# A four-layer graph network on one core: the SBUF start of the adjacency matrices and of the attention matrix is shifted by 64 bytes against the other matmul operands

## The chip, the cores and the metric

The program runs on one core of a Trainium2 chip. Its time is the device time of one execution in microseconds (us); before the change the median of three runs is 2620.7 us (2620.21 to 2622.87). A lower number is better.

## The reference

The input is 64 graphs of 256 nodes with 512 features, and for each graph a 256x256 matrix `adj`. Four layers follow one another, each with a layer norm, a clip at zero and a residual addition:

```
h = relu(layernorm(x))
L0:  Wh = h W;  e = leaky_relu(Wh a1 + (Wh a2)^T);  p = softmax(where(adj > 0.5, e, -9e15), axis=1)
     x = x + elu(p Wh)
L1:  Ah = adj + I;  d = rsqrt(rowsum(Ah));  x = x + relu((d Ah d) h K1 + bias)
L2:  x = x + relu((adj h) K2) * (h has a non-zero in the row)
L3:  x = x + relu(h Wa^T + (adj h / max(rowsum(adj), 1e-6)) Wb^T)
```

Everything is float32 (W, K1, K2, Wa and Wb are 512x512).

## The kernel before

**Split operands.** Every matmul operand is held twice, as a high part (a cast to fp32r) and a low part (what the cast lost). One product is three matmuls: high by high, high stationary by low moving, low stationary by high moving (`product`, lines 273 to 279, all recorded as L277). The first operand of each pair is the stationary one (128 columns, loaded by LDWEIGHTS), the second is the moving one. In the profile's names the moving operand stands first: `O<-w_hi,t_lo` is a matmul that writes O, with w_hi moving and t_lo stationary.

**Matmuls of a layer.** Layers 0 to 2 first gather, then project. `gather` (line 313 on) makes T = (h^T)(adjacency) with a piece of `h_hi`/`h_lo` stationary and 256 columns of `a_hi`/`a_lo` moving (in layer 0 of `p_hi`/`p_lo`, the attention matrix): 4 feature blocks x 2 node blocks x 3 = 24 matmuls 256 wide. `project` (line 347 on) makes O with `t_hi`/`t_lo` stationary and the 512 columns of a weight moving: 24 matmuls 512 wide. Layer 3 turns this round. `transpose_h` transposes h with 8 matmuls (L310, `ident` moving, h stationary); `project_first` multiplies by a weight (T from w and ht, 24 matmuls 512 wide); `gather_last` makes the own term (X from w and ht, 24 of 512), then the gather with `a_hi`/`a_lo` stationary and `t_hi`/`t_lo` moving (O, 12 of 512). `spread` (L298) transposes two vectors.

**Who does the rest.** ScalarE normalises (h), casts h and T to their high parts and applies activations; VectorE computes the low part of T, the statistics and the residual additions of layers 1 and 3; GpSimd computes the low part of h and the residual additions of layers 0 and 2; SyncE issues all DMAs.

**What sets the order.** There is no scheduler. Time is cut in slots j; graph g is in layer n at position 4g + 5n, so four graphs are in flight, one in each layer, and each engine walks the same list of slots in its own written order and waits on semaphores. TensorE's order in a slot is spread, gather or project_first of the next position, transposes, then project or gather_last of this one (lines 378 to 390).

**Where the tensors lie.** All SBUF tensors are allocated once, one behind the other in the order of the `sb(...)` calls (lines 87 to 137), and each starts at the next multiple of 32 bytes of its partition. Two tensors that nothing reads or writes, `distance` (384 bytes a partition) and `p_distance` (192 bytes), hold places apart.

Of the kernel before, what the change touches and what calls it, by code (L numbers as in the profile page):

```python
# [11 lines left out]
P = 128  # L12
# [58 lines left out]
def gnn_kernel(nc, x, adj, adj_t, w_all, a_vecs, bias, out):  # L71
# [8 lines left out]
    with ExitStack() as ctx:  # L80
        def sb(name, shape, dt=F32):
            return ctx.enter_context(nc.sbuf_tensor(name, shape, dt))
# [3 lines left out]

        w_hi = sb("w_hi", [P, WEIGHTS, FT, F], F32R)
        w_lo = sb("w_lo", [P, WEIGHTS, FT, F], F32R)
        distance = sb("distance", [P, 96])
        v_rows = sb("v_rows", [P, 2, F])  # L90
        bias_rows = sb("bias_rows", [P, F])
        ident = sb("ident", [P, P])
# [4 lines left out]
        a_raw = sb("a_raw", [P, A_BUFS, NT, N])  # L97
        a_hi = sb("a_hi", [P, A_BUFS, NT, N], F32R)
        a_lo = sb("a_lo", [P, A_BUFS, NT, N], F32R)
        deg = sb("deg", [P, X_BUFS, NT])  # L100
        deg_one = sb("deg_one", [P, X_BUFS, NT])
        deg_rsqrt = sb("deg_rsqrt", [P, X_BUFS, NT])
# [13 lines left out]
        act_out = sb("act_out", [P, 2, NT, F])  # L116
        scores = sb("scores", [P, NT, N])
        mask_add = sb("mask_add", [P, NT, N])
        p_distance = sb("p_distance", [P, 48])
        p_hi = sb("p_hi", [P, NT, N], F32R)  # L120
        p_lo = sb("p_lo", [P, NT, N], F32R)

# [671 lines left out]
```

## Time and profile before

| | |
|---|---|
| median of 3 runs | 2620.7 us |
| the profiled execution itself | 2621.7 us |
| its span, first to last instruction | 2619.9 us |
| TensorE matmul busy | 2547.1 us (97%) |
| VectorE / ScalarE / GpSimd busy | 1823.2 / 1408.7 / 1185.2 us |
| mean granted TensorE clock | 0.992 |

An engine's busy time is the sum of its instructions' spans. A matmul's recorded span overlaps that of the next one, since matmuls are pipelined; how fast TensorE goes is therefore read from the distance between starts, which the chain of waits in order of time gives directly (so many us for so many matmuls, without overlap).

### The profile page before, as it was taken

How to read it: one execution, taken by the hardware profiler on the slowest of the kernel's cores; microseconds unless marked ns; L12 is line 12 of the kernel's file. 1: busy time of each engine (PE TensorE's matmuls, PEld its weight loads, DVE VectorE, ACT ScalarE, POOL GpSimd, SP SyncE). 2: the span in 40 equal slices, each digit the busy share in tenths (PEclk: the TensorE clock that was granted, in tenths of full speed). 3: DMA queues.
4: the chain of work that ended last, by engine and by line, in shares of the span. 5: the costliest groups of instructions: out<-in, count | busy, mean ns of one | idle time of the engine just before them, and what ended most of it. 6: DMA issues, size and time to landing. Idle time of an engine off the chain costs nothing.

```text
span 2619.9 us, 40393 instructions
## 1 busy us (share of the span) xinstructions
PE 2547.1 (97%) x13704; PEld 2205.5 (84%) x13704; DVE 1823.2 (70%) x4251; ACT 1408.7 (54%) x2571; POOL 1185.2 (45%) x1607
## 2 busy tenths in 40 slices
PE   2799999999999999999999999999999999999998
PEld 2688888888888888888888888888888888888886
DVE  6776676676676677677677777777776766766753
ACT  3555555555555555555555555555555555555542
POOL 2544444444444444444444444444444444444431
PEclk8899999999999999999999999999999999999999
DMA  4101111111011011011111111111111111111000
GB/s 140 41 29 49 33 41 49 33 41 49 30 44 49 29 45 49 29 45 46 33 45 41 37 45 41 37 45 35 42 46 33 41 49 33 41 49 33 29 17 25
DMA packets 72844, 109.30 MB, mean 42 GB/s; under 512 B 4288, under 2 KB 37056, under 8 KB 72640
## 3 DMA queue, kind: packets, MB, share of 16 engines
q1 hardware_dynamic: 72640, 106.71, 12.6%
q8 instruction: 112, 1.84, 0.3%
q14 instruction: 92, 0.75, 0.1%
HBM read 73.14 MB, written 33.55 MB: 41 GB/s over the span
## 4 chain that ended last, share of the span: by engine, by line
PE 96%; DVE 1%; issue 1%; ACT 1%; POOL 1%; DMA 0%; SPq 0%; POOLq 0%; ACTq 0%; DVEq 0%
PE O L277 46%; PE T L277 34%; PE X L277 13%; PE X L310 2%; PE X L298 1%; POOL h_lo L747 0%; ACT h L405 0%; DMA act_out<-w_all 0%; POOL xs L712 0%; DVE p_lo L589 0%; DVE scores L522 0%; DVE w_lo L512 0%; DVE t_lo L595 0%; ACT act_out L436 0%; DVE xs L630 0%
## 5 line engine op out<-in xcount | busy, mean ns | idle before, releaser
L747 POOL TENSOR_TENSOR h_lo<-h,h_hi 128x512 fp32r<-128x512 f32 x384 | 503.4, 1333 | 673.1 <-ACT h_hi L411 673.1
L595 DVE TENSOR_TENSOR t_lo<-T,t_hi 128x512 fp32r<-128x512 f32 x512 | 352.5, 690 | 399.1 <-ACT t_hi L417 399.1
L405 ACT ACTIVATE h<-xs,ln_bias,ln_scale 128x512 f32<-128x512 f32 x512 | 396.0, 811 | 391.9 <-POOL ln_bias L741 391.9
L277 PE MATMUL O<-w_hi,t_hi 128*128 128x512 f32 x1536 | 603.2, 393 | 0.0
L277 PE MATMUL O<-w_hi,t_lo 128*128 128x512 f32 x1536 | 598.2, 389 | 0.0
L277 PE MATMUL O<-w_lo,t_hi 128*128 128x512 f32 x1536 | 598.1, 389 | 0.0
L417 ACT CAST t_hi<-T 128x512 fp32r<-128x512 f32 x512 | 298.3, 584 | 257.1 <-PE T L277 257.1
L712 POOL TENSOR_TENSOR xs<-xs,act_out 128x512 f32<-128x512 f32 x128 | 163.7, 1297 | 531.7 <-ACT act_out L439 496.9
L277 PEld LDWEIGHTS O<-w_hi,t_lo 128*128 128x128 f32 x1536 | 288.3, 188 | 60.2
L277 PEld LDWEIGHTS O<-w_hi,t_hi 128*128 128x128 f32 x1536 | 288.5, 188 | 55.9 <-DVE t_lo L595 0.5
L277 PEld LDWEIGHTS O<-w_lo,t_hi 128*128 128x128 f32 x1536 | 288.6, 188 | 55.7
L540 DVE BATCH_NORM_STATS2 ln_stats<-xs 128x6 f32<-128x512 f32 x512 | 326.7, 678 | 11.4 <-POOL xs L718 5.5
L277 PE MATMUL T<-a_hi,h_hi 128*128 128x256 f32 x1024 | 288.2, 281 | 3.0 <-DVE t_lo L595 3.0
L277 PE MATMUL T<-a_hi,h_lo 128*128 128x256 f32 x1024 | 287.8, 281 | 0.0
L277 PE MATMUL T<-a_lo,h_hi 128*128 128x256 f32 x1024 | 287.7, 281 | 0.0
L411 ACT CAST h_hi<-h 128x1024 fp32r<-128x1024 f32 x192 | 201.8, 1051 | 109.2 <-PE T L277 107.2
L277 PE MATMUL T<-w_hi,ht_hi 128*128 128x512 f32 x512 | 205.4, 401 | 4.2 <-DVE ht_lo L602 4.2
L277 PE MATMUL T<-w_lo,ht_hi 128*128 128x512 f32 x512 | 200.2, 391 | 0.0
L277 PEld LDWEIGHTS T<-a_hi,h_hi 128*128 128x128 f32 x1024 | 192.4, 188 | 9.1 <-issue 3.7
L277 PE MATMUL T<-w_hi,ht_lo 128*128 128x512 f32 x512 | 200.0, 391 | 0.0
L277 PE MATMUL X<-w_hi,ht_hi 128*128 128x512 f32 x512 | 199.2, 389 | 0.0
L277 PE MATMUL X<-w_lo,ht_hi 128*128 128x512 f32 x512 | 199.2, 389 | 0.0
(92 smaller groups left out, 4991.4 us busy)
## 6 DMA issues: line engine op xcount, KB each, us to landing
xs<-x SPq DMA_DIRECT2D x64, 512.0 KB, 3.6
out<-xs SPq DMA_DIRECT2D x64, 512.0 KB, 2.8
a_raw<-adj_t SPq DMA_DIRECT2D x64, 256.0 KB, 2.7
a_rows<-adj SPq DMA_DIRECT2D x64, 256.0 KB, 2.7
xs<-w_all SPq DMA_DIRECT2D x6, 512.0 KB, 7.3
act_out<-w_all SPq DMA_DIRECT2D x2, 512.0 KB, 6.7
z<-w_all SPq DMA_DIRECT2D x2, 512.0 KB, 6.4
v_rows<-a_vecs SPq DMA_DIRECT2D x1, 512.0 KB, 5.4
```

The costliest lines, as they stand in the source:

```text
L277: last = nc.tensor.matmul(psum, s, m, start=(start and n == 0 and i == 0), stop=(stop and n == len(pairs) - 1 and i == 2))
L298: last = nc.tensor.transpose(wh_rows[:, m * P:m * P + P], wh[:, k.g % 2, 0, m:m + 1].to_broadcast([P, P]), ident[:])
L310: last = nc.tensor.transpose(X[:, half, c:c + P], h[:, k.odd, m, f * P:f * P + P], ident[:])
L405: nc.scalar.activation(h[:, k.odd, m], xs[:, k.xb, m], ACT.Relu, bias=ln_bias[:, k.quad, m:m + 1], scale=ln_scale[:, k.quad, m:m + 1], acc ...
L411: nc.scalar.copy(h_hi[:, k.odd], h[:, k.odd]).then_inc(h_hi_ready, 1)
L417: nc.scalar.copy(t_hi[:, k.odd, c], T[:, c]).then_inc(t_hi_ready, 1)
L540: nc.vector.bn_stats(ln_stats[:, k.quad, m], xs[:, k.xb, m]).then_inc(stats_ready, 1)
L595: nc.vector.tensor_tensor(t_lo[:, k.odd, c], T[:, c], t_hi[:, k.odd, c].bitcast(F32), ALU.subtract).then_inc(t_lo_ready, 1)
L712: nc.gpsimd.tensor_tensor(xs[:, k.xb, n], xs[:, k.xb, n], act_out[:, 0, n], ALU.subtract).then_inc(pool_added, 1)
L747: nc.gpsimd.tensor_tensor(h_lo[:, k.odd, m], h[:, k.odd, m], h_hi[:, k.odd, m].bitcast(F32), ALU.subtract).then_inc(h_lo_ready, 1)
```

## The change

Three sizes of unused tensors: the one behind the weights (renamed) grows from 96 to 112 elements, a new one of 112 elements stands behind `a_lo`, and the one ahead of `p_hi` grows from 48 to 64. Nothing else differs: every engine's instructions, with their waits, stand in the same order as before.

```
-        distance = sb("distance", [P, 96])
+        w_distance = sb("w_distance", [P, 112])
...
         a_lo = sb("a_lo", [P, A_BUFS, NT, N], F32R)
+        a_distance = sb("a_distance", [P, 112])
         deg = sb("deg", [P, X_BUFS, NT])
...
-        p_distance = sb("p_distance", [P, 48])
+        p_distance = sb("p_distance", [P, 64])
```

What becomes of the start addresses (bytes within a partition, worked out from the sizes in the order of allocation; the first weight starts at 16512):

| tensor | start before | start after | place before, modulo 512 | place after, modulo 512 |
|---|---|---|---|---|
| w_hi, w_lo | 16512, 57472 | the same | 128 | 128 |
| ident | 104960 | 105024 | 0 | 64 |
| xs | 105536 | 105600 | 64 | 128 |
| a_raw, a_hi, a_lo | 130112, 138304, 146496 | each + 64 | 64 | 128 |
| h, h_hi, h_lo | 158080, 166272, 174464 | each + 512 | 384 | 384 |
| t_hi, t_lo, ht_hi, ht_lo | 182656, 190848, 199040, 203136 | each + 512 | 384 | 384 |
| z, act_out, scores, mask_add | 207232 to 221568 | each + 512 | 384 | 384 |
| p_hi, p_lo | 223808, 225856 | each + 576 | 64 | 128 |

So in absolute bytes h, t and ht do move, by 512; modulo 512 they stay. The blocks that a matmul takes out of these tensors start at multiples of 512 bytes from the tensor's start, so each block has its tensor's place modulo 512.

## Rows read from the trace of the kernel before

**Rows 1.** The page's busy times, and the granted clock in 40 slices.
```profile
PE 2547.1 (97%) x13704; PEld 2205.5 (84%) x13704; DVE 1823.2 (70%) x4251; ACT 1408.7 (54%) x2571; POOL 1185.2 (45%) x1607
...
PEclk8899999999999999999999999999999999999999
```

**Rows 2.** The chain that ended last, 200 to 2600 us, by line.
```profile
by line: PE O L277 48.0%; PE T L277 35.0%; PE X L277 14.0%; PE X L310 2.2%; PE X L298 0.5%; DVE ht_lo L602 0.1%; DVE xs L630 0.1%; DVE z L627 0.0%; DVE t_lo L595 0.0%; ACT t_hi L417 0.0%; issue 0.0%; DVEq L193 0.0%
```

**Rows 3.** TensorE's waits, 200 to 2600 us: total us, times, longest.
```profile
PE T L277 <- DVE ht_lo L602: 4.2, 2, 2.5
PE T L277 <- DVE t_lo L595: 0.2, 1, 0.2
```

**Rows 4.** The chain from 1011 to 1042 us: start, us, engine, matmuls.
```profile
1011.19 5.47 PE O L277 x24
1016.66 0.22 PE X L298 x2
1016.88 5.46 PE T L277 x24
1022.34 5.44 PE O L277 x24
1027.78 2.83 PE T L277 x24
1030.60 5.44 PE X L277 x24
1036.04 2.75 PE O L277 x12
1038.79 2.83 PE T L277 x24
```

**Rows 5.** TensorE's matmuls by form, 200 to 2600 us: count, busy us, mean ns.
```profile
L277 PE MATMUL O<-w_lo,t_hi 128*128 128x512 f32 x1440 | 560.8, 389 | 0.0
L277 PE MATMUL T<-a_hi,h_lo 128*128 128x256 f32 x968 | 272.1, 281 | 0.0
L277 PE MATMUL T<-p_hi,h_hi 128*128 128x256 f32 x464 | 130.4, 281 | 0.0
L277 PE MATMUL O<-t_lo,a_hi 128*128 128x512 f32 x248 | 97.7, 394 | 0.0
L277 PE MATMUL O<-t_hi,a_hi 128*128 128x512 f32 x248 | 97.2, 392 | 0.0
L277 PE MATMUL O<-t_hi,a_lo 128*128 128x512 f32 x248 | 96.3, 388 | 0.0
L310 PE MATMUL X<-ident,h 128*128 128x128 f32 x496 | 64.2, 272 | 0.0
```

**Rows 6.** TensorE's instructions in order of time from 136.66 us: start, us.
```profile
136.66 0.36 PE L277 MATMUL T<-a_hi,h_hi 128*128 128x256 f32 x1 [2.24 <-DVE t_lo L595]
136.85 0.28 PE L277 MATMUL T<-a_lo,h_hi 128*128 128x256 f32 x1
...
137.44 0.28 PE L277 MATMUL T<-a_hi,h_hi 128*128 128x256 f32 x1
137.55 0.28 PE L277 MATMUL T<-a_lo,h_hi 128*128 128x256 f32 x1
...
139.48 0.27 PE L310 MATMUL X<-ident,h 128*128 128x128 f32 x1
```

**Rows 7.** The same view at 62 us, and the window table (fourth number: granted clock).
```profile
62.10 0.41 PE L277 MATMUL T<-p_hi,h_lo 128*128 128x256 f32 x1
62.31 0.41 PE L277 MATMUL T<-p_hi,h_hi 128*128 128x256 f32 x1
...
61.30:64.10 2.80, 2.80 (x15) 0.50 0.00 0
```

**Rows 8.** The same view from 35.62 us, behind a stop of TensorE.
```profile
35.62 0.39 PE L277 MATMUL O<-w_lo,t_hi 128*128 128x512 f32 x1
35.85 0.40 PE L277 MATMUL O<-w_hi,t_lo 128*128 128x512 f32 x1
36.09 0.39 PE L277 MATMUL O<-w_hi,t_hi 128*128 128x512 f32 x1
36.32 0.40 PE L277 MATMUL O<-w_lo,t_hi 128*128 128x512 f32 x1
```

## The prediction

> **What bounds the kernel now.** I read the busy times first, then the chain that ended last, then TensorE's waits, and only then single matmuls. TensorE is busy 97% of the span, the next engine 70%, and the granted clock is 0.9 or more from the third slice on [rows 1]. Between 200 and 2600 us the chain is 99.7% TensorE, nearly all of it the line that issues every product [rows 2]; in these 2400 us TensorE waits for others 4.4 us in all [rows 3]. So the time is the sum of the distances between matmul starts, and nothing that the change does to another engine counts unless it is large. What is left to ask is whether the same matmuls run at a different pace from other addresses.
>
> **The pace of a matmul.** The chain in order of time shows one round of layers [rows 4]. 24 matmuls of 512 columns with weights moving take 5.44 us, 226.7 ns each. 24 of 256 columns in a gather take 2.83 us, 117.9 ns each, where half of 226.7 would be 113.3. The 12 matmuls of 512 columns of the last gather, with t moving and the adjacency matrix stationary, take 2.75 us, 229.2 ns each, where 12 x 226.7 would be 2.72. So two kinds of product run above the pace of the weight products: the gathers by 4.5 ns a matmul, the last gather by 2.5 ns. The mean spans agree: 281 ns for both kinds of gather, 389 for the weight products, 392, 394 and 388 in the last gather [rows 5].
>
> Is 113.3 ns reachable at 256 columns, or is a narrow matmul simply dearer? One gather tells. It began after a wait of 2.24 us; from its seventh matmul at 137.44 to its end at 139.48 there are 18 matmuls in 2.04 us, 113.3 ns each [rows 6]. They are the same instructions, at the same addresses, without the 4.5 ns. So the excess is a stall in a repeating phase between what TensorE reads as moving data and what it reads as the next stationary block, and a phase without it exists at this width. And at the half clock, 0.50 granted, starts lie 0.21 us apart [rows 7], which is 256 columns at 1.2 GHz with nothing on top: the excess belongs to reading at full speed.
>
> What sets the phase that holds? The kinds of product differ in where their two operands lie. Modulo 512 bytes, stationary minus moving, from the table of addresses:
> - weights moving, t or ht stationary: 384 - 128 = 256, no excess (x24 in 5.44 us) [rows 4];
> - a or p moving, h stationary: 384 - 64 = 320, excess 4.5 ns;
> - t moving, a stationary: 64 - 384 = 192 (modulo 512), excess 2.5 ns on average.
>
> The last is the telling one: it has the weight products' width, stationary size and engine, and differs in its distance (and in the tensors). The weight products have blocks at many different multiples of 512 and all run at the same pace, so I take 512, or a divisor of it, as the period.
>
> **The change, part by part.** After it a, p and w share one place (128), and h, t and ht another (384). All three kinds of product then have the distance 256, in one direction or the other, which is the distance without an excess.
>
> (1) Gathers. Between 200 and 2600 us there are 968 / 8 = 121 with a and 464 / 8 = 58 with p, 179 in all [rows 5], since each form occurs 8 times in a gather. Of the 13 others I count 8 at full clock and full excess; the rest are in the start, at half clock, or the one above. Each saves 2.83 - 2.72 = 0.11 us: 187 x 0.11 = 20.6 us. Rounding of the rows allows 19.5 to 21.5. From below the bound is nothing saved; from above I know no lower pace than 113.3.
>
> (2) Last gathers: 64 x (2.75 - 2.72) = 1.9 us saved.
>
> (3) Transposes of h: `ident` moves and h does not, so stationary minus moving goes from 384 to 320, the distance at which the gathers lose. These matmuls are fp32, eight of them in a quarter of the gathers' number of groups. If they took the gathers' 4.5 ns, 512 x 4.5 = 2.3 us would be lost; if they have slack between reads, nothing. The weight groups behind them take 5.47 and 5.46 us instead of 5.44 [rows 4], a few disturbed starts that a new phase could lengthen or remove: 128 x 0.03 = 3.8 us is the bound either way. I take + 0.6 us for both.
>
> (4) The other engines read and write at places shifted by 64 or 512 bytes. Their work lies beside TensorE's (at least 30% idle each), TensorE waits 4.4 us for them in 2400 [rows 1, 3], and the gathers' saving of 0.11 us in a slot asks little of that slack. The single blocks at the seams change their distance too, weights moving with a stationary from 448 to 0, 64 times; at the few ns that such seams show, under 0.5 us. Nothing for both.
>
> (5) The start (some 140 us, with TensorE waiting) and the last 20 us hold mostly other engines' work and half-clock stretches, where I leave everything as it is.
>
> Sum: - 20.6 - 1.9 + 0.6 = - 21.9 us. Against the profiled execution's 2621.7 us that gives 2599.8; that execution was 1.0 us above the median of the runs, so for a median I forecast 2599 us.
>
> The Trainium skill has a rule against this. Its page "SBUF — State Buffer", section "A bandwidth-pool intuition that's wrong (but worth ruling out)", gives TensorE a second, independent read port for LDWEIGHTS, and the section "SBUF: two separate sides" says that TensorE never waits on anyone there. By that the two streams can't meet, and an address can't change the pace: 2620.7. The trace bears it out for the weight products and at the half clock, and does not for the gathers, where equal instructions run at 117.9 and 113.3 ns.
>
> **The rivals.**
> - Nothing happens, 2620.7 (2619 with the last gathers alone). The phase would be set by the rhythm of 256-column matmuls with 128-column loads, whatever the distance: a gather that starts in step with the matmuls ahead falls into the slow phase, one that starts after a wait does not. For it: the fast and the slow phase occur at one address. Against it: a and p gathers, which follow different groups, have the same 281 ns, and the last gather has an excess at 512 columns. This is also the case in which the ports are independent, and in which the change does to the addresses what it says and nothing hangs on it.
> - Part of it, 2606. The high and low parts come in threes, and in the last gather two of three have an excess (392 and 394, against 388) while the third has none. If one matmul of three still meets its load at 256, a third of the 20.6 us stays: 2599 + 7 = 2606. For it: the threes in [rows 5]. Against: the weight products have the same threes and no such pattern.
> - Slower, 2640. At the new distance the gathers could hold the phase that the weight products pass through after a stop: starts at 35.62, 35.85, 36.09 and 36.32, which is 0.23 to 0.24 us apart, up to some 9 ns above their pace [rows 8]. The weight products leave it within a few matmuls; if the shorter ones stay in it, each of 187 x 24 = 4488 is 9 ns above 113.3 instead of 4.5, and the time is 2620.7 + 4488 x 4.5 ns = 2641. It is slower from the point at which the gathers' excess is over 4.5 ns. Against it: the weight products start thousands of times at this distance, from all kinds of neighbours, and settle each time.
>
> **How the numbers follow.** The forecast (both gathers at the weight products' pace) gets 0.76, part of it 0.08, nothing 0.10, slower 0.06. Faster by over 0.2% (5.2 us, about what a measurement of this kernel tells from no change) comes with the first two, 0.84; the same 0.10; slower 0.06. The forecast's own range is 2595 to 2603: the rounding of (1) and the 2.3 and 3.8 us of (3) on both sides. The range to hold 8 in 10 takes in the partial case with its own margin, 2595 to 2611, and leaves out no change and slower, 0.16 together.
>
> **What would show it.** In the chain after the change, every x24 gather should take 2.72 us where 2.83 stood, the x12 group 2.72 where 2.75 stood, and the weight groups 5.44 as before; mean spans should be 277 in the gathers instead of 281, and about 389 in all three forms of the last gather. The transposes' 272 ns tell whether the distance 320 harms them. TensorE's waits for others should stay at a few us in 200 to 2600. I am wrong if the gathers keep 2.83 us (then distance is not what sets the phase), or if the saving there shows up again as waits or in the groups behind the transposes.

## The result, and the profile after

The changed kernel takes 2629.1 us (median of 8 runs, 2628.6 to 2629.2) beside 2621.1 us before: ratio 1.0028, 95% interval 1.0017 to 1.0039. It is slower by 8 us, where I forecast 22 us faster. The profiled execution took 2629.2 us, its span 2627.4.

The page, busy times: TensorE has 8.0 us more than in [rows 1], VectorE and ScalarE are within 1 us of what they had, and GpSimd is 4.5 us lower.

```profile
PE 2555.1 (97%) x13704; PEld 2213.8 (84%) x13704; DVE 1823.8 (69%) x4251; ACT 1407.8 (54%) x2571; POOL 1180.7 (45%) x1607
```

The chain in order of time (start, us, engine and line, matmuls), one round of layers, to be held against [rows 4]. Lines are one higher than before (L278 for L277).

```profile
1005.21 5.47 PE O L278 x24
1010.68 2.87 PE T L278 x24
1013.55 0.88 PE X L311 x8
1014.43 5.46 PE O L278 x24
1019.89 0.22 PE X L299 x2
1020.11 5.46 PE T L278 x24
1025.56 5.44 PE O L278 x24
1031.00 2.87 PE T L278 x24
1033.87 5.47 PE X L278 x24
1039.34 2.72 PE O L278 x12
1042.06 2.87 PE T L278 x24
```

Four things changed. A gather takes 2.87 us for 2.83. The weight products right behind a gather (1005.21 and 1033.87) take 5.47 for 5.44. The last gather takes 2.72 for 2.75, as forecast. The weight products behind the transposes (1014.43) take 5.46 for 5.47. The mean spans by form, 200 to 2600 us, agree when held against [rows 5]: 282 or 283 for 281 in the gathers, 389 for 394 in the last gather, 272 as before in the transposes.

```profile
L278 PE MATMUL T<-a_hi,h_lo 128*128 128x256 f32 x968 | 273.9, 283 | 0.0
L278 PE MATMUL T<-p_hi,h_lo 128*128 128x256 f32 x464 | 131.3, 283 | 0.0
L278 PE MATMUL O<-t_lo,a_hi 128*128 128x512 f32 x244 | 94.9, 389 | 0.0
L311 PE MATMUL X<-ident,h 128*128 128x128 f32 x488 | 63.2, 272 | 0.0
```

TensorE's waits did not change. Between 200 and 2600 us one of the two waits of [rows 3] is missing, but only because the run is later by then and that wait comes after 2600 us (first line: 200 to 2600 us; second line: 2600 us to the end). Over the whole run both kernels wait 4.2 us there, in two waits. Nothing came back through another engine.

```profile
PE T L278 <- DVE ht_lo L603: 1.7, 1, 1.7
PE T L278 <- DVE ht_lo L603: 2.5, 1, 2.5
```

One more difference isn't tied to the addresses by any run. Near the end, behind a wait of 2.5 us in both traces, the granted clock fell to 0.50 before the change and stayed at 1.00 after it, and a group of weight products took 7.38 and 5.74 us. Of the traces of the 20 kernels 12 have this stretch (before and all64 do, the changed kernel and a_only don't). Before (a line of the chain and one of the window table, fourth number: granted clock), then after:

```profile
2598.86 7.38 PE T L277 x24
2601.00:2603.00 2.00, 2.00 (x7) 0.50 0.00 0
2608.01 5.74 PE T L278 x24
```

The sum, from the starts of all matmuls in both traces: the gathers + 8.7 us (by the starts one is 2.872 for 2.827; 187 x 0.045 is 8.4, the rest is in the start and at the end); the 124 weight groups right behind gathers + 3.4 (0.028 each); last gathers 64 x 0.027 = - 1.7; the 62 weight groups behind transposes - 0.8; the stretch at the half clock - 1.6; waits and start - 0.5. Together + 7.5, which is what the span grew by.

### The profile page after: what moved, and what is told of

Same layout as the page of the kernel before. It is cut to its first block, busy times and chain, and to the rows that moved or that the text cites. A ratio compares the mean times of both kernels' runs of the same rounds, so it can differ in the third digit from the quotient of the medians.

```text
span 2627.4 us, 40393 instructions
## 1 busy us (share of the span) xinstructions
PE 2555.1 (97%) x13704; PEld 2213.8 (84%) x13704; DVE 1823.8 (69%) x4251; ACT 1407.8 (54%) x2571; POOL 1180.7 (45%) x1607
## 4 chain that ended last, share of the span: by engine, by line
PE 95%; DVE 1%; issue 1%; ACT 1%; POOL 1%; DMA 0%; SPq 0%; POOLq 0%; ACTq 0%; DVEq 0%
PE O L278 45%; PE T L278 34%; PE X L278 13%; PE X L311 2%; PE X L299 1%; ACT h L406 0%; POOL h_lo L748 0%; DMA act_out<-w_all 0%; POOL xs L713 0%; DVE p_lo L590 0%; DVE ln_stats L541 0%; DVE scores L523 0%; DVE w_lo L513 0%; DVE t_lo L596 0%; DVE a_lo L662 0%
## 5 line engine op out<-in xcount | busy, mean ns | idle before, releaser
L278 PE MATMUL O<-w_hi,t_hi 128*128 128x512 f32 x1536 | 604.5, 394 | 0.0
L278 PE MATMUL O<-w_lo,t_hi 128*128 128x512 f32 x1536 | 598.2, 389 | 0.0
L278 PE MATMUL O<-w_hi,t_lo 128*128 128x512 f32 x1536 | 597.8, 389 | 0.0
L278 PEld LDWEIGHTS O<-w_hi,t_lo 128*128 128x128 f32 x1536 | 288.3, 188 | 61.2
L278 PEld LDWEIGHTS O<-w_hi,t_hi 128*128 128x128 f32 x1536 | 288.8, 188 | 56.1 <-DVE t_lo L596 0.5
L278 PEld LDWEIGHTS O<-w_lo,t_hi 128*128 128x128 f32 x1536 | 288.9, 188 | 55.3
L278 PE MATMUL T<-a_hi,h_hi 128*128 128x256 f32 x1024 | 289.7, 283 | 2.9 <-DVE t_lo L596 2.7
L278 PE MATMUL T<-a_lo,h_hi 128*128 128x256 f32 x1024 | 289.8, 283 | 0.0
L278 PE MATMUL T<-a_hi,h_lo 128*128 128x256 f32 x1024 | 289.7, 283 | 0.0
L278 PE MATMUL T<-w_hi,ht_hi 128*128 128x512 f32 x512 | 204.6, 400 | 4.2 <-DVE ht_lo L603 4.2
L278 PEld LDWEIGHTS T<-a_hi,h_hi 128*128 128x128 f32 x1024 | 196.2, 192 | 8.6 <-issue 3.6
L278 PEld LDWEIGHTS T<-a_lo,h_hi 128*128 128x128 f32 x1024 | 196.2, 192 | 4.8
L278 PE MATMUL X<-w_hi,ht_hi 128*128 128x512 f32 x512 | 200.0, 391 | 0.0
L278 PE MATMUL X<-w_lo,ht_hi 128*128 128x512 f32 x512 | 199.9, 390 | 0.0
L278 PE MATMUL T<-w_lo,ht_hi 128*128 128x512 f32 x512 | 199.5, 390 | 0.0
```

The costliest lines, as they stand in the source:

```text
L278: last = nc.tensor.matmul(psum, s, m, start=(start and n == 0 and i == 0), stop=(stop and n == len(pairs) - 1 and i == 2))
```

## The experiments

All of them move tensors by unused ones and change nothing else. "Place" is a start modulo 512, "distance" stationary minus moving; "weight products" are the groups with a weight moving, and the "seam" is where one group follows another, so that the first block of the new one is loaded beside the last moving data of the old one. Each edit stands as a diff against the kernel before; for the later runs, which differ in sizes alone, as the elements a partition of each unused tensor (before: `distance`, here w_distance, 96; p_distance 48; none behind a_lo or h_lo).

**Is it the place or the distance?** First everything 64 bytes later, the weights too:

```
+        front = sb("front", [P, 16])
         w_hi = sb("w_hi", [P, WEIGHTS, FT, F], F32R)
```

> Every tensor of before, the weights too, starts 64 bytes later; all distances between operands are those of before. Theory D (the pace of a matmul follows the distance modulo 512 between its stationary and its moving operand): nothing changes, 24-matmul gathers at 2.83 us, last gather 2.75, time within 1.5 us of before. Theory P (the pace follows the place of an operand itself, a and p at 128 instead of 64): gathers at 2.87 us as after the change, time near 2629 us.

Measured 2621.2 us, ratio 0.9998 (0.9988 to 1.0007), every group of the chain as before. Theory P is out: a and p lay at 128 as after the change, and the gathers kept 2.83. Theory D, the distance, holds so far.

Then the change without its part at p:

```
-        distance = sb("distance", [P, 96])
+        w_distance = sb("w_distance", [P, 112])
+        a_distance = sb("a_distance", [P, 112])        # behind a_lo
```

> The change without its part at p: a, xs and ident 64 bytes later, p where it was (place 64 modulo 512), h and t at 384. Theory D: gathers with a 2.87 us, gathers with p 2.83, last gather 2.72; 128 gathers cost 0.045 us more (5.8), the groups behind them some 0.03 us each for two groups of a round (up to 3.6), the last gather gives 1.7 back: 2626 to 2629 us. Theory P says the same of the gathers. A theory by which p alone is to blame says before's time, 2621.

Measured 2626.3 us, ratio 1.0017 (1.0007 to 1.0026), in the range. In its chain the p gather at 1028.83 and the weight group behind it are as before, the a gathers as after the change.

```profile
1023.39 5.44 PE O L278 x24
1028.83 2.83 PE T L278 x24
1031.65 5.44 PE X L278 x24
1037.09 2.72 PE O L278 x12
1039.81 2.87 PE T L278 x24
```

Then all but the weights 64 bytes later:

```
-        distance = sb("distance", [P, 96])
+        w_distance = sb("w_distance", [P, 112])
```

> All but the weights 64 bytes later: a and p at 128, h, t, ht at 448, weights at 128. Theory D: gathers keep 2.83 us (distance 320) and the last gather 2.75 (distance 192) although a and p lie where the change put them; the weight products go to distance 320, untried, and leave 5.44 us: by the gathers' row at 320 (117.8 - 106.7 = 11.1 ns a matmul over the width at 2.4 GHz, against 13.3 at 256) to 5.39 us if the excess belongs to the load of the stationary operand, some 2600 us in all; if the excess goes with the width they become slower, 5.66 us, some 2690 us. Theory P: gathers 2.87, weight products 5.44.

Measured 2652.4 us (two runs), ratio 1.0115. The weight products went to 5.59 and 5.60 us: they follow distance. Both sizes that I named for them were wrong. And the gathers, at 320 as before, took 2.73 to 2.75 us; once settled their matmuls start every 113.4 ns, the pace of the forecast:

```profile
1012.56 5.59 PE O L277 x24
1018.15 2.73 PE T L277 x24
1020.88 0.87 PE X L310 x8
...
1033.17 5.60 PE O L277 x24
1038.77 2.73 PE T L277 x24
```

One distance, two paces of a gather. Distance alone doesn't settle it; what ran ahead counts too. On theory D this is half a failure.

**How the pace depends on distance.** h448 moves h (t and ht with it) and p; the other three move a and p and leave h and t at their place modulo 512.

```
h448:       w_distance 96, a_distance 16, no p_distance
a96_p32:    w_distance 104, a_distance 120, p_distance 40
a0_p160:    w_distance 80,  a_distance 16,  p_distance 72
a192_p256:  no w_distance,  a_distance 96,  p_distance 96
```

> a stays at 64 as before, h, t and ht at 448, p at 448. Distances: a gathers 384, p gathers 0, weight products 320, last gather 128. Theory D: weight products at the pace of the run with all but the weights shifted; a and p gathers now differ from each other, each at a pace of its own; no size forecast for 384, 0 and 128, between 106.7 ns (no excess) and 125 ns a matmul. Theory P: a gathers as before, 2.83.

> Weights, h and t as before (weight products at distance 256), a at place 96 and p at 32: gathers with a at distance 288, gathers with p at 352, last gather at 224. Theory L (each load of a stationary block takes cycles from the moving stream; how many follows the distance and the phase in which the products ahead leave the two): weight products keep 5.44 us, the two gathers differ from 2.83, each in one of the states seen so far (2.72 fast, 2.83, 2.87) or between. Theory R (only the phase that the weight products leave counts, the distance of the gather itself does not): both gathers 2.83.

> As the run with a at 96, but a at 0 and p at 160: gathers with a at distance 384, with p at 224, last gather at 128. At 384 the gathers took 2.84 us where weight products ran at 320. Theory L: 2.72 to 2.87, not bound to 2.84. If a distance alone decides, without phase: 2.84 again. If the period were 128 bytes instead of 512, a at distance 384 would behave as at 256: 2.87.

> a at 192 and p at 256: gathers with a at distance 192, with p at 128, last gather at 320. If the order of the two streams doesn't count, 192 is 320 mirrored: gathers with a in 2.72 or 2.83, and the last gather (a stationary) in 2.72 to 2.75. Else open between 2.67 (a stall of half the 26.7 cycles now) and 3.0 us.

Measured 2675.8 (h448), 2632.0 (a96_p32), 2631.8 (a0_p160) and 2632.5 us (a192_p256). Theory R is out: in the last three the weight products ahead of the gathers kept 5.44, and the gathers took between 2.80 and 2.88 us, by their own distance. A period of 128 doesn't fit either: at 384 a gather took 2.85 or 2.88, not 2.87 each time with the even 120.0 ns of 256. The chain of a0_p160 shows a at 384 behind the last gather and behind weights, then p at 224:

```profile
1002.39 2.85 PE T L278 x24
1005.24 5.47 PE O L278 x24
1010.71 2.88 PE T L278 x24
...
1025.61 5.44 PE O L278 x24
1031.05 2.80 PE T L278 x24
```

**What is the period?** Now the weight products' distance too.

```
w384:       w_distance 96, a_distance 32, p_distance 112
a320_p320:  w_distance 32, a_distance 64, p_distance 112
w224:       w_distance 24, a_distance 64, p_distance 120
w192:       w_distance 16, a_distance 64, p_distance 112
w0:         w_distance 96, a_distance 64, p_distance 112
```

> h, t, ht at 0, a at 64 as before, p at 448: weight products at distance 384, gathers at 448 and 64, last gather at 64. Theory L: weight products at a pace that is neither forced to 5.44 (256) nor 5.60 (320); the farther from 256 the worse, by the two points known, so 5.60 to 5.9, some 2690 us or more. If the period is 128, weight products are back at 5.44 and the gathers at 2.83.

> Weights, h and t as before; a and p both at place 320, so both gathers at distance 64, the last gather at 448. Where the weight products ran at 384, a gather at 64 held 113.4 ns a matmul. Theory L with the distance deciding: gathers 2.72 to 2.75 us, 188 x 0.1 = 19 us less; weight products behind them at most 0.04 us more in two groups of a round (5); last gather up to 2.80 (3 more): 2605 to 2612. Theory R (the phase left by weight products at 256 decides): 2.83 and up, 2621 to 2632.

> Weight products at distance 224, gathers at 64 (a) and 32 (p), last gather at 448. It tells how wide the good place of the weight products at 256 is. If the stall comes only when two reads come within some 16-byte rows of each other, 224 still gives 5.44 us; if 256 is a point, 5.5 to 5.6 and some 2640 us.

> Weight products at distance 192, the mirror of 320, gathers at 64. If only the gap between the two streams counts, 5.60 us as at 320 (2650 us in all). If the side counts too, some other value between 5.4 and 5.7.

> Weight products at distance 0, gathers at 64. If the period is 256 bytes, 5.44 us. If 0 is the place farthest from 256, the worst of all: 5.6 to 5.9 us, 2650 to 2740 in all. The single blocks of before that had distance 0 (t moving, h loaded) showed no excess over 226.7 ns, which speaks for the first.

Measured 2661.7 (w384), 2621.3 (a320_p320), 2657.5 (w224), 2638.4 (w192) and 2621.3 us (w0). In w384 the weight products took 5.58 to 5.60 us at 384 where they take 5.44 at 256, which settles that the period is not 128. Two of these kernels have the time of the one before (ratios 1.0000, 0.9991 to 1.0009, and 1.0000, 0.999 to 1.001), group by group. a320_p320 has the gathers at 64 instead of 320 and the last gather at 448 instead of 192; w0 in addition has the weight products at 0 instead of 256. What they share with before is the distance modulo 256, for all three kinds of product. My "from the run at 384 a gather at 64 is fast" failed, for the same reason as the forecast. The chain of a320_p320:

```profile
1021.54 5.44 PE O L278 x24
1026.98 2.83 PE T L278 x24
1029.81 5.44 PE X L278 x24
1035.25 2.75 PE O L278 x12
```

With that period the groups of all runs so far go into one table (us; medians of about 60 groups from the starts, or the spread over groups of different entry):

| distance modulo 256 | weight products, 24 x 512 | gather, 24 x 256 | last gather, 12 x 512 |
|---|---|---|---|
| 0 | 5.44 | 2.87 | 2.72 |
| 32 | not run | 2.84 | not run |
| 64 | 5.60 | 2.83, or 2.73 to 2.75 | 2.79 to 2.80 |
| 96 | not run | 2.85 | not run |
| 128 | 5.58 to 5.60 | 2.84 to 2.88 | 2.78 to 2.80 |
| 192 | 5.49 to 5.51 | 2.83 | 2.75 to 2.77 |
| 224 | 5.60 | 2.80 | 2.79 |

The weight products were not run at 32 and 96. Products of 512 columns are best at 0, gathers nearly worst. At 64 a gather has two paces: 117.7 ns where the weight products ran at 0 or 192, 113.4 ns where they ran at 64, 128 or 224.

**What chooses between the two?** Two runs give h a place of its own. The gathers stay at 64 and the weight products at 0, and what changes for a gather is the seam (the first load of h beside the last moving block ahead). The first is the changed kernel with its new tensor moved:

```
h_own448:
-        a_distance = sb("a_distance", [P, 112])        # behind a_lo, as after the change
+        t_distance = sb("t_distance", [P, 112])        # behind h_lo
h_own64 (against before):
         w_distance 80, a_distance 64, t_distance 80 (behind h_lo), p_distance 32
```

> The changed kernel with its new tensor behind h_lo instead of behind a_lo: a, p at 128 and t, ht at 384 as after the change, h alone at 448. By the period of 256 bytes that the runs show: weight products 0 (5.44 us), last gather 0 (2.72), gathers at 64, and the first load of a gather beside a weight block at 64. The gathers at 64 held 117.7 ns where the weight products ran at 0 or 192, and 113.4 where they ran at 64, 128 or 224. If what decides is the weight products' own rhythm (which is that of distance 0 here): 2.83, and only the last gather's 1.7 us are won, 2619 us. If the load at the seam decides: 2.73, and 188 x 0.1 us more are won, about 2600 us.

> h at 64, a and p at 0, t and ht at 384: weight products 0, gathers 64, the load at the seam of weights and gather at 192, the last gather at 128. The last gather costs 2.78 to 2.80 (3 us more in all). Gathers by the weight products' rhythm 2.83, about 2624 us; by the seam open, 2.73 to 2.83, so 2605 to 2624.

Measured 2622.5 us, ratio 1.0004 (0.9995 to 1.0013), and 2618.8 us, ratio 0.9990 (0.9980 to 1.0001). In h_own448 the gathers are back at 2.83. `ident` and `xs` lie there as after the change, so the changed kernel's loss in the gathers goes with the distance of h to a and p alone. The last gather has 2.72. The seam didn't bring the fast pace.

```profile
1029.74 2.83 PE T L278 x24
1032.57 5.47 PE X L278 x24
```

The weight group behind the gather keeps its 5.47 us. By its starts the first five matmuls take 233, 236, 228, 233 and 231 ns and the others 227, much as in the changed kernel (233, 236, 228, 232, 231), although the gather ahead has the pace of before. What these two kernels share, and the one before does not, is the seam with t: its first block is loaded beside a moving a or p block at distance 256, where before it was 320. In h_own64 one gather of each round did become fast, the one behind the last gather, which there runs at distance 128 (2.79):

```profile
1027.02 2.83 PE T L279 x24
1029.85 5.45 PE X L279 x24
1035.30 2.79 PE O L279 x12
1038.09 2.73 PE T L279 x24
```

Its addresses are those of the other a gathers, and the load at its seam stands at 192 as behind the weights; what differs is the rhythm ahead. Together with w_fixed64 this says that a gather inherits its state from the group before it.

**Can a gather behind weight products at 0 be brought to the fast pace?** h_lo gets its own place (a tensor ahead of it, another behind it that puts t back modulo 256):

```
hlo64:   lo_distance 16 ahead of h_lo, t_distance 48 behind it
hlo128:  lo_distance 32, t_distance 32
hlo192:  lo_distance 48, t_distance 16
```

> Only h_lo moves against before, by 64 (modulo 256): in a gather the loads of high blocks stay at distance 64 from the moving data, the load of the low block stands at 128. If each load is charged by its own distance and phase, the gathers leave the even 117.7 ns and show a pattern of three, between 2.73 and 2.88 us; a kick that throws them into the other state gives 2.73 and some 2602 us. If the group's state is set once at its entry, they keep 2.83.

> As the run before, with h_lo 128 on: the low load at distance 192. At 192 alone the gathers held 117.7, so I expect 2.80 to 2.85 unless the change of phase helps them into the fast state (2.73).

> As the run before, with h_lo 192 on: the low load at distance 0. At 0 alone the gathers held 120.0. One of three loads at 0 and two at 64: 118.5, or 2.84 us, if they add up one by one; some 2625 us.

Measured 2628.5 (hlo64), 2610.2 (hlo128) and 2629.3 us (hlo192); for hlo128 the ratio is 0.9958 (0.9939 to 0.9978). Each load counts by its own distance. With low blocks at 128 (hlo64) the starts leave the even pattern (2.84 us). With low blocks at 192 (hlo128) the gathers stumble for six matmuls and then hold 113.4 ns, 2.75 us in all. I had given that one chance among others. With low blocks at 0 (hlo192) they take 2.83, not the 2.84 of adding up, and the weight groups behind them lose, 5.48 to 5.49, as they do in hlo64 (5.47). In both the seam with t is that of before, modulo 256, so the rhythm that a gather leaves counts there as well. The first starts of a gather in hlo128, and later ones:

```profile
1003.14 0.28 PE L279 MATMUL T<-a_hi,h_hi 128*128 128x256 f32 x1
1003.26 0.28 PE L279 MATMUL T<-a_lo,h_hi 128*128 128x256 f32 x1
1003.38 0.28 PE L279 MATMUL T<-a_hi,h_lo 128*128 128x256 f32 x1
...
1004.19 0.28 PE L279 MATMUL T<-a_hi,h_hi 128*128 128x256 f32 x1
1004.31 0.28 PE L279 MATMUL T<-a_lo,h_hi 128*128 128x256 f32 x1
1004.42 0.28 PE L279 MATMUL T<-a_hi,h_lo 128*128 128x256 f32 x1
```

The last run joins this to what the change did give:

```
-        distance = sb("distance", [P, 96])
+        w_distance = sb("w_distance", [P, 112])
+        lo_distance = sb("lo_distance", [P, 32])       # ahead of h_lo
+        t_distance = sb("t_distance", [P, 80])         # behind h_lo
-        p_distance = sb("p_distance", [P, 48])
+        p_distance = sb("p_distance", [P, 64])
```

> The changed kernel's places for the weights (128), a and p (128) and t, ht (384), so weight products and last gather at distance 0, with h_hi at 448 and h_lo at 64 modulo 512: in the gathers high loads at 64 and low loads at 192, as in the run that got 2610.2 us. If distances modulo 256 and the state at entry are all there is: gathers 2.75 us, last gather 2.72 (1.7 us less in all), groups behind the gathers between 5.44 and 5.47: 2608 to 2611 us. If the gathers' fast state needs more than its distances (the places of ident or xs, which move by 64), 2.83 and some 2622.

Measured 2606.2 us, ratio 0.9946 (0.9933 to 0.9960): faster than both kernels, and 2 us better than expected. The gathers settle a little sooner, 2.74 us for the 2.75 of hlo128, which is 2 us in all. Its chain:

```profile
1017.06 5.44 PE O L279 x24
1022.50 2.74 PE T L279 x24
1025.24 5.46 PE X L279 x24
1030.71 2.72 PE O L279 x12
1033.43 2.74 PE T L279 x24
```

## Why the prediction was wrong

- **The bound** was right: TensorE's starts are the time. The whole difference lies in its groups.
- **"Half of 226.7 would be 113.3"** is the step that failed. I read the weight products as free of a stall and their 226.7 ns as a price that goes with the width. At distance 0 modulo 256, which the change gave all products, a matmul of 512 columns takes 226.7 ns and one of 256 takes 120.0. Over the width at 2.4 GHz (213.3 and 106.7) both pay 13.3 ns, 32 cycles: there the charge is one per matmul, not per column. Each matmul has one load of a 128-column block, and the hlo runs show that each load's distance counts, so I put the charge on the load; that last step is argued. It is equal for the two widths at this distance only: at 64 it is 20 ns for 512 columns and 6.7 or 11.0 for 256. My own list had the warning, since 5.44/24 over the bare width is 13.3 ns and 2.83/24 is 11.2: read per matmul, the weight products were the dearer kind. But those rows fit either reading, and no row had 256 columns at distance 256. Moving the gathers there costs 120.0 - 117.8 = 2.2 ns x 4488 = 10 us. It was 8.4 by the chain, as the first two starts of each gather still lie 113 ns apart. So term (1) was + 8.4 instead of - 20.6.
- **The 113.3 ns of [rows 6]** exists, and belongs to before's distance of 320 (64 modulo 256), not to the weights' 256. I joined a pace found at one distance with another distance. What it needs was shown by runs: distance 64 with a fitting rhythm ahead, or low blocks at 192.
- **Distance, not place**, was right (all64), and so was **term (2)**: the last gather went to 2.72, 1.7 us of the 1.9. There the argument compared equal widths, which is why it held. The period is 256 bytes, one of the divisors of 512 that I had left open.
- **Term (3)**: the transposes keep 272 ns at 320, and the weight groups behind them gave 0.8 us back where I had + 0.6 for both. Small, as I had it.
- **Term (4), the seams**, which I put at nothing, cost 3.4 us. I had counted only the 64 seams of weights and a. The ones that cost are those of a gather and the weight products behind it, which went from 320 to 256: the first five matmuls of the group then take 28 ns more together. h_own448 and the last run have the same seam and the same loss behind gathers of 2.83 and 2.74 us, so the slower gather ahead isn't needed for it.
- **The rival "nothing happens"** had one part right: the rhythm of the group ahead chooses between two paces of a gather (w_fixed64, h_own64). "Whatever the distance" was wrong.
- **The slower rival** had the sign and not the size: I priced a gather at 9 ns over 113.3, the runs show 6.7. My lower bound, "nothing saved", was no bound: by the row of the weight products, read per matmul, the gathers could lose.
- **The Trainium skill's** "SBUF — State Buffer", section "A bandwidth-pool intuition that's wrong (but worth ruling out)", gives LDWEIGHTS an independent read port. If that means that the addresses of the two operands can't slow each other, the traces do not agree: shifting one operand by 64 bytes against the other took the weight products from 5.44 to 5.60 us (w_fixed64). My sentence that the trace bears the page out for the weight products rested on the same misreading of their 226.7 ns.

What stays open is the mechanism inside: the runs show a period of 256 bytes, a charge for each load, and states that are inherited. They don't show which parts of the memory the two reads meet in, nor why a gather settles at 113.4 or 117.7. They also don't give a rule for the seams: distance and rhythm both count there.

## What to carry to other kernels

Where TensorE never waits, the distance between starts less the bare width is a price for each matmul. Work it out per matmul for every width before taking one kind as the clean one, and don't carry a price from one width to another without a run: what was best for 512 columns was nearly worst for 256. Start addresses can be worth half a per cent to the good and two per cent to the bad in this kernel. Try the distances of stationary and moving operands modulo 256 bytes in steps of 32, for each width apart and for the high and the low operand apart, and look at the groups behind as well.

## What the runs showed of the hardware

- fp32r matmuls at a granted clock of 1.00 (2.4 GHz), back to back with a load of 128 columns each, took 13.3 ns over their width at distance 0 modulo 256, for 512 and for 256 columns. At 512 columns it was 15.6 ns at 192 and 20 ns at 64. At 256 columns it was 6.7 or 11.0 ns at 64. At the half clock there was no excess at 256 columns and distance 64 [rows 7].
- Moving all operands together by 64 bytes changed nothing (ratio 0.9998).
- One product at one distance can run at two steady paces (117.7 and 113.4 ns). The group ahead chooses, and the pace holds to the end of the group.
- Behind a gather whose seam with the next group stood at distance 256, the first five matmuls of that group took 28 ns more together, with gathers of 2.87, 2.83 and 2.74 us ahead; at 320 behind 2.83 they took none.
